# A state layer's step products in one pass, its input and modulation partly on ScalarE, and a new order in its recurrence

## What is computed

```python
# layer 0: time-mixing attention with its own FFN, then 8 experts of capacity 128
x = x + ga * attn0(mod(layernorm(x)));   x = x + gb * switch_moe(mod(layernorm(x)))
# layer 1, the state layer (it is what most of the change is about)
xb, z = in_proj(mod(layernorm(x)))                       # 128 -> 256 and 256
u = silu(conv4(xb) + conv_b)
dt_raw (8), b (16), c (16), gate (256) = x_proj(u)
dt = softplus(dt_raw @ dt_proj + dt_b)                   # the step products
a = -exp(A_log) * (0.5 + sigmoid(gate))
for each token, each state n of 16:
    s[n] = exp(dt * a[n]) * s[n] + dt * b[n] * u
    y += s[n] * c[n]
x = x + ga * out_proj((y + D * u) * silu(z))
# then 16 experts (top 8, dense) and one shared expert of width 128
x = x + gb * (sum_e w_e * down_e(silu(gate_e h) * up_e h) + shared(h))
```

## Time and profile before

| | |
|---|---|
| median of 3 runs | 700.81 us (699.96 to 701.22) |
| the profiled execution | 701.86 us, its span 700.1 us |
| mean granted TensorE clock | 0.917 of full speed |
| busy: PE, DVE, ACT, POOL | 584.9, 555.8, 389.9, 406.5 us |
| chain that ended last | PE 34%, DVE 33%, issue 15%, POOL 11%, ACT 6% |

### The profile page before, as it was taken

The page is one execution under the profiler, slowest core; times in us unless marked ns, Lnnn a source line. Parts: engine busy times, 40 slices in busy tenths (PEclk is TensorE's granted clock), DMA queues, the critical chain, the costliest instruction groups (busy, mean ns, idle before and its releaser), DMA issues.

```text
span 700.1 us, 6733 instructions
## 1 busy us (share of the span) xinstructions
PE 584.9 (84%) x1896; PEld 325.1 (46%) x1896; DVE 555.8 (79%) x728; ACT 389.9 (56%) x664; POOL 406.5 (58%) x345
## 2 busy tenths in 40 slices
...
GB/s 304 12 1 1 0 1 0 320 0 0 2 61 61 0 1 0 45 1 0 0 0 23 22 23 45 24 11 2 45 1 0 167 107 79 134 116 137 119 114 15
DMA packets 14597, 34.96 MB, mean 50 GB/s; under 512 B 1952, under 2 KB 2240, under 8 KB 14080
## 3 DMA queue, kind: packets, MB, share of 16 engines
...
...
## 4 chain that ended last, share of the span: by engine, by line
PE 34%; DVE 33%; issue 15%; POOL 11%; ACT 6%; DMA 1%; POOLq 0%; DVEq 0%; SPq 0%; ACTq 0%
PE ps L985 11%; DVE arena L1716 11%; POOL h_parts L1923 6%; DVE arena L1691 6%; PE ps L648 5%; POOL arena L1796 4%; DVE arena L1484 3%; PE ps L927 2%; PE ps L811 2%; PE ps L859 2%; DVE ps L1468 2%; PE ps L778 2%; DVE ps L1643 1%; DVE place L1599 1%; PE ps L874 1%
## 5 line engine op out<-in xcount | busy, mean ns | idle before, releaser
L1796 POOL TENSOR_TENSOR arena<-arena 128x512 f32<-128x512 f32 x184 | 225.8, 1253 | 45.9 <-DVE arena L1716 28.1
L1716 DVE TENSOR_TENSOR_SCAN arena<-ps,carry,arena 128x512 f32<-128x512 f32 x128 | 156.6, 1266 | 0.0
L1345 ACT ACTIVATE ps<-arena,abase 128x512 f32<-128x512 f32 x128 | 88.5, 692 | 78.7 <-DVE arena L1716 77.7
L1923 POOL TENSOR_TENSOR h_parts<-arena,h_parts 128x512 fp32r<-128x512 f32 x68 | 100.0, 1487 | 51.3 <-ACT h_parts L1379 51.3
L927 PE MATMUL ps<-arena,core 128*128 128x512 f32 x256 | 127.8, 622 | 0.4 <-POOL arena L1796 0.3
L985 PE MATMUL ps<-x_parts,w_hi 128*128 128x512 f32 x272 | 100.7, 410 | 0.9 <-DVE arena L1691 0.9
L1691 DVE TENSOR_TENSOR arena<-ps,arena 128x1024 f32<-128x1024 f32 x64 | 77.0, 1203 | 11.2 <-PE ps L1023 11.2
L1023 PE MATMUL ps<-bc,sel 96*128 96x512 bf16 x128 | 44.5, 403 | 41.8 <-DVE arena L1691 31.6
L1789 DVE TENSOR_TENSOR arena<-arena 128x512 f32<-128x512 f32 x64 | 72.5, 1133 | 2.2
L927 PEld LDWEIGHTS ps<-arena,core 128*128 128x128 f32 x256 | 50.6, 198 | 41.3 <-issue 29.2
L1784 DVE TENSOR_TENSOR arena<-ps,arena 128x512 f32<-128x512 f32 x68 | 46.5, 684 | 22.0 <-PE ps L985 11.2
...
## 6 DMA issues: line engine op xcount, KB each, us to landing
...
```

Source lines behind the costliest of these rows:

```text
L1345: A(bank(6 + c), ch(DTG[:, c, :], i), ACT.Exp, scale=ABASE[:, c * NS + n:c * NS + n + 1]).then_inc(*done(f"dec{n}_{c}", i))
L1716: nc.vector.tensor_tensor_scan(ST[:, k % ST_RING, :], bank(6 + c), DBU[:, (2 * q + c) % DBU_RING, :], CARRY[:, k:k + 1], ALU.mult, ALU.add ...
L1796: mul = lambda o, a, b: nc.gpsimd.tensor_tensor(o, a, b, ALU.mult)
L1923: nc.gpsimd.tensor_tensor(HWP[:, 1, q % 4, :], (HW if e < E1 else HH)[:, q % H_RING, :], HWP[:, 0, q % 4, :].bitcast(f32), ALU.subtract).t ...
```

## The change

1. In the FFN stage `centreD(i-2)` goes behind `up3(i)`; in the tail `varD(0)` and `varD(1)` go ahead of `centreD(2)` and `centreD(3)`, and ACT and DVE follow this order.
2. `combine` of chunk 0 is split: experts 0 to 3 behind `e_down(6)`, 4 and 5 behind `e_down(7)`, 6 and 7 where all stood.
3. `modE` and `xb1_scaled` go from DVE to ACT, with a new order on ACT.
4. The step products: instead of an fp32 product of 8 rows, one fp32r pass of 24 rows that holds the high and low parts of data and weights (x high, x low, x high against w high, w high, w low). ACT writes `dt_hi` instead of `dt_raw_copy`, and once `dt_w_hi`; DVE writes `dt_parts` (four times 24x512) and once `dt_w`. The `bc` product gets 120 rows instead of 104.
5. `z(0)` moves behind `gate1(0)`: `z0` ahead of `bc(2)`, `z1` behind it; their silu on ACT behind `gate1_tanh` and behind `u(3)`; `dt(0)` waits for them.
6. The diagonal of D comes in the weights' transfer (256 columns more in `wC`) instead of from ACT at turn 1. `Du(0)` goes ahead of turn 0, the other `Du` to turns 18, 19, 34, 50 and 51.
7. In the second recurrence the side steps of a chunk move: ACT's gates one turn earlier; `y_copy` +2 (was +3), POOL's `gated` +1 (was +2), `m_out` in two halves at +5 and +6, `centreF` in two at +7 and +8, `sqF` +7 (+8), `varF` +9 (+10), `rsF` +9 (+10), `normF` +10 (+9), `g_act` +12 (+13).
8. In the last stage `hh` of a routed expert is written in place in its PSUM bank, and `hw` reads PSUM and the weight row; `up_product(m)` then waits for `hw(m-2)`.

```diff
-    "pe": by_turn(chain("pe", [(6, "m_out"), (8, "centreF"), (10, "varF"), (13, "g_router")]),
-                  [(62, "g_router", 1), (47, "g_turn", 0), (NQ + 9, "g_turn", 1), (NQ + 15, "g_turn", 2), (NQ + 28, "g_turn", LAST)],
-                  [(NQ + 8, "m_out", LAST), (NQ + 11, "centreF", LAST), (NQ + 13, "varF", LAST), (NQ + 17, "g_router", LAST)]),
-    "act": by_turn([(1, "diag", 0)], chain("act", [(3, "y_copy"), (6, "gam"), (8, "sqF"), (10, "rsF"), (11, "modF"), (12, "x_hi"), (13, "g_act")]),
-                   [(63, "g_act", 1), (48, "turned", 0), (NQ + 10, "turned", 1), (NQ + 16, "turned", 2), (NQ + 29, "turned", LAST)],
+    "pe": by_turn(chain("pe", [(5, "m_half"), (6, "m_out"), (7, "centre_x"), (8, "centreF"), (9, "varF"), (13, "g_router")]),
+                  [(18, "Du0", 1), (19, "Du1", 1), (34, "Du0", 2), (50, "Du0", LAST), (51, "Du1", LAST)],
+                  [(62, "g_router", 1), (45, "g_turn", 0), (NQ + 9, "g_turn", 1), (NQ + 15, "g_turn", 2), (NQ + 28, "g_turn", LAST)],
+                  [(NQ + 8, "m_half", LAST), (NQ + 8, "m_out", LAST), (NQ + 11, "centreF", LAST), (NQ + 13, "varF", LAST), (NQ + 17, "g_router", LAST)]),
+    "act": by_turn(chain("act", [(2, "y_copy"), (6, "gam"), (7, "sqF"), (9, "rsF"), (11, "modF"), (12, "g_act"), (12, "x_hi")]),
+                   [(63, "g_act", 1), (46, "turned", 0), (NQ + 10, "turned", 1), (NQ + 16, "turned", 2), (NQ + 29, "turned", LAST)],
                    [(NQ + 11, "sqF", LAST), (NQ + 14, "rsF", LAST), (NQ + 16, "modF", LAST), (NQ + 18, "g_act", LAST), (NQ + 19, "x_hi", LAST)]),
-    "dve": by_turn(chain("dve", [(9, "normF")]), [(NQ + 5, "gated", LAST), (NQ + 9, "x_mamba", LAST), (NQ + 15, "normF", LAST)],
+    "dve": by_turn(chain("dve", [(10, "normF")]), [(NQ + 5, "gated", LAST), (NQ + 9, "x_mamba", LAST), (NQ + 15, "normF", LAST)],
                    [(start + k // pace, f"gating{k}", i) for i, (start, pace) in enumerate(((28, 1), (NQ + 1, 4), (NQ + 6, 1), (NQ + 20, 1))) for k in range(4)]),
-    "pool": by_turn(chain("pool", [(2, "gated"), (7, "x_mamba"), (12, "x_lo")]), [(NQ + 20, "x_lo", LAST)]),
+    "pool": by_turn(chain("pool", [(1, "gated"), (7, "x_mamba"), (12, "x_lo")]), [(NQ + 20, "x_lo", LAST)]),
...
-GATE_ACT = {2: ("gate", 0, 1), 3: ("gate", 1, 1), 4: ("gate", 0, 2), 6: ("gate", 1, 2), 8: ("gate", 0, 3), 10: ("gate", 1, 3),
-            11: ("z", 0, 2), 12: ("z", 1, 2), 13: ("z", 0, 3), 14: ("z", 1, 3), 15: ("z", 0, 1), 16: ("z", 1, 1)}
+GATE_ACT = {1: ("gate", 0, 1), 2: ("gate", 1, 1), 3: ("gate", 0, 2), 5: ("gate", 1, 2), 7: ("gate", 0, 3), 9: ("gate", 1, 3),
+            10: ("z", 0, 2), 11: ("z", 1, 2), 12: ("z", 0, 3), 13: ("z", 1, 3), 14: ("z", 0, 1), 15: ("z", 1, 1)}
...
-            pe += [("up0", i), ("up1", i)] + ([("centreD", i - 2)] if i >= 2 else []) + [("up2", i), ("up3", i)]
+            pe += [(f"up{f}", i) for f in range(NF)] + ([("centreD", i - 2)] if i >= 2 else [])
...
-    add(pe, [("centreD", 2), ("varD", 0), ("centreD", 3), ("varD", 1), ("varD", 2), ("varD", 3)])
+    add(pe, [("varD", 0), ("varD", 1), ("centreD", 2), ("centreD", 3), ("varD", 2), ("varD", 3)])
...
+COMBINE_AFTER = {E0 - 2: range(4), E0 - 1: range(4, E0 - 2)}
...
     for e in range(E0):
-        pe += [("e_down", e)] + ([("e_up", e + 2)] if e + 2 < E0 else [])
+        pe += [("e_down", e)] + ([("e_up", e + 2)] if e + 2 < E0 else []) + [(f"combine{j}", 0) for j in COMBINE_AFTER.get(e, ())]
...
-    add(pe, combine(0), combine(1), [("centreE", 0)], combine(2), [("varE", 0), ("centreE", 1)], combine(3), [("varE", 1)], xb(0),
-        [("centreE", 2), ("varE", 2)], xb(1), [("centreE", 3), ("varE", 3)], xb(2), xb(3), z(0),
-        [("bc", 0), ("gate0", 0), ("bc", 1), ("gate1", 0), ("bc", 2)], dt(0), [("bc", 3)], dt(1), dt(2), dt(3))
-    add(act, [("sqE", 0)], ln_rs(0), [("sqE", 1)], ln_rs(1), xb_copy(0), [("sqE", 2)], ln_rs(2), xb_copy(1), [("sqE", 3)], ln_rs(3), one("a_exp"),
-        xb_copy(2), u(0), xb_copy(3), z_silu(0), raw(0), u(1), [("gate0_tanh", 0)], raw(1), u(2), [("gate1_tanh", 0)], raw(2), u(3),
-        [("bc_mid", 0)], sp(0), raw(3), [("bc_mid", 1)], sp(1), [("bc_mid", 2), ("bc_mid", 3)], sp(2), sp(3))
+    raw, sp = (lambda i: [("bc_hi", i), ("dt_hi", i)]), (lambda i: [("sp_0", i), ("sp_1", i)])
+    add(pe, [(f"combine{j}", 0) for j in range(E0 - 2, E0)], combine(1), [("centreE", 0)], combine(2), [("varE", 0), ("centreE", 1)], combine(3), [("varE", 1)], xb(0),
+        [("centreE", 2), ("varE", 2)], xb(1), [("centreE", 3), ("varE", 3)], xb(2), xb(3),
+        [("bc", 0), ("gate0", 0), ("bc", 1), ("gate1", 0), ("z0", 0), ("bc", 2), ("z1", 0)], dt(0), [("bc", 3)], dt(1), dt(2), dt(3), [("Du0", 0), ("Du1", 0)])
+    add(act, [("sqE", 0)], ln_rs(0), [("sqE", 1), ("modE", 0)], ln_rs(1), xb_copy(0), [("sqE", 2), ("modE", 1)], ln_rs(2), xb_copy(1), [("sqE", 3), ("modE", 2)], ln_rs(3),
+        one("a_exp", "dt_w_hi"), xb_copy(2), [("modE", 3)], u(0), xb_copy(3), raw(0), u(1), [("gate0_tanh", 0)], raw(1), u(2), [("gate1_tanh", 0), ("z0_silu", 0)], raw(2),
+        u(3), [("z1_silu", 0), ("bc_mid", 0)], sp(0), raw(3), [("bc_mid", 1)], sp(1), [("bc_mid", 2), ("bc_mid", 3)], sp(2), sp(3))
+    norm_e = lambda i: [("normE", i)]
+    rest = lambda i: [("bc_r1", i), ("dt_parts", i)]
     add(dve, [("kept_x", 0), ("kept_x", 1)], sums(0), places(3), one("xb_zero"), [("kept_x", 2)], sums(1), norm_e(0), [("kept_x", 3)], sums(2), norm_e(1), sums(3), conv(0, 0), norm_e(2), conv(1, 0), norm_e(3),
-        conv(0, 1), conv(1, 1), conv(0, 2), conv(1, 2), [("bc_r1", 0)], conv(0, 3), conv(1, 3), one("a_neg", "st_zero"), [("bc_r1", 1), ("bc_r1", 2), ("bc_r1", 3)],
+        conv(0, 1), conv(1, 1), one("dt_w"), conv(0, 2), rest(0), conv(1, 2), conv(0, 3), rest(1), conv(1, 3), one("a_neg", "st_zero"), rest(2), rest(3),
...
+        return ([("Du1", 2)] if (j, y) == (2, 0) else []) + [(f"y{y}_{c}", j) for c in range(DI)]
...
-                x_proj(half(1, i, BC3 + DTR), i, DI * P, BC3 + DTR).then_inc(*done("bc", i))
+                x_proj(half(1, i, DT3.stop), i, DI * P, DT3.stop).then_inc(*done("bc", i))
+
+            def z(c):
+                a = wc_at["in"][0] + (DI + c) * P
+                pe.wait_ge(*upto(f"gate{c}_tanh", 0))
+                mm(half(c, 0), wC[:, a:a + P], ch(HC, 0), start=True, stop=True).then_inc(*done(f"z{c}", 0))
 
             def dt(i):
-                a = wc_at["dtp"][0]
-                pe.wait_ge(*upto("dt_raw_copy", i))
-                for c, w in enumerate(([], ["bc_r1"]) if i else (["gate0_tanh"], ["gate1_tanh"])):
-                    for name in w:
-                        pe.wait_ge(*upto(name, i))
-                    mm(half(c, i), wC[BC3:BC3 + DTR, a + c * P:a + (c + 1) * P], ch(DRAW, i)[BC3:BC3 + DTR],
-                       start=True, stop=True).then_inc(*done(f"dt{c}", i))
+                pe.wait_ge(*upto("dt_parts", i))
+                for c in range(DI):
+                    if i == 0:
+                        pe.wait_ge(*upto(f"z{c}_silu", 0))
+                    mm(half(c, i), DT_W[:, c * P:(c + 1) * P], ch(DT_X, i), start=True, stop=True).then_inc(*done(f"dt{c}", i))
...
             bc(0)
-            pe.wait_ge(*upto("z1_silu", 0))
             x_proj(half(0, 0), 0, 0, P).then_inc(*done("gate0", 0))
             bc(1)
-            pe.wait_ge(*upto("dt_raw_copy", 0))
-            pe.wait_ge(*upto("bc_r1", 0))
+            pe.wait_ge(*upto("dt_parts", 0))
             x_proj(half(1, 0), 0, P, P).then_inc(*done("gate1", 0))
+            z(0)
             bc(2)
+            z(1)
             dt(0)
             bc(3)
...
+            def d_u(c, i):
+
+                if i == 0:
+                    pe.wait_ge(*upto("sp_0", c))
+                elif i == 1:
+                    pe.wait_ge(*upto(f"z{c}_half", 1))
+                elif i == 2:
+                    pe.wait_ge(*(upto("g_w", 0) if c else upto("lnF", 0)))
+                else:
+                    pe.wait_ge(*(upto("normF", 1) if c else upto("g_turned", 0)))
+                mm(bank(c + 2 * (i % 2)), DIAG(c), ch(U[:, c, :], i), start=True, stop=False).then_inc(*done(f"Du{c}", i))
...
+            def m_half(i):
+                out_product(0, i, "m_half")
+
             def m_out(i):
-                a = wc_at["out"][0]
-                for c in range(DI):
-                    pe.wait_ge(*upto(f"gated_{c}", i))
-                    last = mm(bank(2 * (i % 2)), wC[:, a + c * P:a + (c + 1) * P], ch(U[:, c, :], i), start=(c == 0), stop=(c == DI - 1))
-                last.then_inc(*done("m_out", i))
+                out_product(1, i, "m_out")
+
+            def out_product(c, i, step):
+                a = wc_at["out"][0] + c * P
+                pe.wait_ge(*upto(f"gated_{c}", i))
+                mm(bank(2 * (i % 2)), wC[:, a:a + P], ch(U[:, c, :], i), start=(c == 0), stop=(c == DI - 1)).then_inc(*done(step, i))
...
-                pe.wait_ge(*(expert("hh{}", m - 2) if m >= 2 else upto(f"st{NS - 1}_{m}", NCH - 1)))
```

(19 more changed lines are left out.)

150 lines of the change are left out of this document (77 added, 73 removed).

## The result

| | before | after |
|---|---|---|
| median | 701.01 us (699.96 to 702.19, 4 runs) | 682.91 us (678.79 to 683.93, 4 runs) |
| the profiled execution | 701.86 us, span 700.1 | 678.79 us, span 677.0 |
| ratio to before | 1 | 0.973 (95% interval 0.9686 to 0.9775) |
| mean granted clock | 0.917 | 0.939 |

The forecast was 681 us, range 676 to 690. The profiled execution is the fastest of the four. Timed again on another occasion, the same kernel had a median of 682.05 us in 6 runs, against 701.47 us of the kernel before in 11; the ratio was 0.9717 (0.9683 to 0.975).

The account below looks back on a forecast made before the run. The bound changes by stage: DVE in the recurrence, PE in the last stage, no engine full in the projections. Terms -2.6 -4.0 +1.2 -3.4 -9.4 -1.3 = -19.5 us from the 700.81 median gave 681 us, range 676 to 690.

Parts of the forecast that it names:

- FFN and layernorm D, -2.6: FFN stage: PE's two idle times before `centreD`, 2.6 us together, both go; bounds 0 and -2.6.
- Sums, -4.0: Layer 0's expert sums: 12 of the first 16 products go ahead, so `moe_sum(0)` starts earlier, -4.0 us.
- the better bound: Sums of layer 0's experts: -4.5 us, if the last expert's product coming 0.6 us later is hidden.
- Projections, +1.2: Layernorm E to step products: ACT becomes the bound with 5.8 us more work, softplus ends 1.2 later; bounds -0.5, +5.8.
- The rival of ACT's queue (+5.8): Projections: ACT's queue costs all the work it gets, +5.8 instead of +1.2, total 685.9 us; chance 0.13.
- Step products: End of projections: PE's 4.6 us saved are worth nothing by themselves, but make room for `Du(0)` ahead of turn 0.
- Start, -3.4: Recurrence's first turns: earlier gates, no `diag` on ACT and `Du` ahead recover 3.4 of 3.9 us; bounds -1.0, -3.9.
- Recurrence, -9.4: Second recurrence: DVE's five waits, 10.1 us, go except 0.7, the three before `normF` being 7.5; bounds -3 and -10.
- The 1.42 us: Recurrence: DVE's wait before turn 38's `dbu`, put down to `Du` and side products on PE, expected to go.
- the rival: Recurrence: POOL or a ring takes over, gain 3 us instead of 9.4, total 687.7 us; chance 0.15.
- Last stage, -1.3: Last stage, PE-bound: `hw` at 0.69 us halves PE's 1.86 before `g_router(3)`, plus 0.4 for clock and tail; bounds 0, -3.
- The clock: Rival: new small waits lower PE's clock in sums, projections and last stage, giving back 1.5 + 0.5 + 1.3 us: 684.6; chance 0.07.

Follow-up runs that it names:

- the first trace: First profiled execution of the changed kernel, all parts in, beside the kernel before: 678.79 us, span 677.0.
- the second: Trace of the changed kernel timed again on another occasion, no edit: median 682.05 us, ratio 0.9717, span 681.7.

## Why the prediction was right, point by point

- **As a whole.** The errors of the terms partly cancel, which is luck: the projections cost 1.2 to 1.4 us more than forecast and the last stage gave 1.0 more. By the medians 18.1 and 19.4 us were gained, against 19.5.
- **FFN and layernorm D, -2.6.** Right: -2.7, and 2.6 us of waits return when the step goes back.
- **Sums, -4.0.** Right in mechanism: -4.5, +4.6 when undone. The last expert's product was to come 0.6 us late. It comes 0.5 late, but the last `y_lo` does not (13.98 us behind the first, 13.97 before), so the better bound held.
- **Projections, +1.2.** The sign held; the size was half of the +2.4, and the account of it failed. The term took ACT's moved work for the bound, ACT busy some 36 of 38 us; it was 32.6. With that work back on DVE the stage is no shorter (59.1), although the first `u` is 2.8 us earlier. The comparison is not quite of like with like, since `bc(3)` ran at the lower clock there, which goes with 60.2 to 60.9 us elsewhere. What remains is order: `u(i+1)` stands on ACT behind two copies that wait for PE's product of `u(i)`, once a chunk; the remainders `rest(0)` wait on DVE ahead of a convolution (3.07 us, at 270.15 in the timeline of DVE after); and `dt(0)` waits for z1's silu. With the first two taken apart and chunk 3's modulation on DVE the stage is at 56.6, the length of before; what each of these gives was not separated, except 1.2 us for the modulation. The rival of ACT's queue (+5.8) fails with it. The fifth part, which moves z, had no term and was not undone alone.
- **Step products.** Priced at nothing by themselves, and twice as many cost nothing. That they gave `Du(0)` its room was argued only, and the fourth part as a whole was not undone.
- **Start, -3.4.** The number was right in the first trace (-3.9), less so in the second (-2.7), and the mechanism is only partly shown. Of the 3.9, 1.2 are the clock between the two traces of the same code. Putting the gates and the D products back returns 1.4. The other 1.3 no run separates; the diagonal, which the experiment left in the transfer, is one candidate. So the experiment's rival, the diagonal or the clock, is true in part.
- **Recurrence, -9.4.** Right: -9.1, and 8.7 when undone. Its main argument, that `normF` one turn later outlasts each wait, was tried alone and took all 7.5 us, at the price of 2.4 us of new waits that the changed kernel does not have. The 1.42 us were blamed on the wrong thing: the wait is before the `dbu` of turn 41, not 38, and it comes back with the side steps, not with `Du`. POOL was busy 52.8 of 56 us and never held DVE up: the rival is out.
- **Last stage, -1.3.** Mechanism right, size short: -2.3, and when undone 2.8 by the medians and 3.8 in the stage. The prediction took half of PE's 1.86 us; 1.7 went, and with it the stretch at the lower clock. `normF(3)` comes 0.9 us earlier behind the first `hh` (38.06 against 38.93). By the trace `hw` is 0.69 us, as priced, and the longer wait of `up_product` shows as 0.4 us in all.
- **The clock.** Of the rival's case the part in the projections came (0.88 us a product behind the 4.94 us wait). In the sums it did not: 24 products take 5.88 us, 0.25 each. The larger effect was in no term: between two executions of the same code 3.0 us in one stretch and 1.2 in another.
